# Two-layer graph network on one core: the row-picking one-hots compare two half-precision operands in SBUF

## The reference, cut to what matters

```
def _rel_layer(h, src, dst, etype, norm, V, comp, loop_w, bias, activation):
    c = comp[etype]
    for b in range(num_bases):
        xb = h @ V[b]
        m = m + c[:, b, None] * xb[src]
    agg = segment_sum(m * norm, dst)
    out = agg + bias + h @ loop_w
...
h = maximum(layernorm(x), 0);  x = x + relational layers 0 and 1 of h
h = maximum(layernorm(x), 0);  x = x + gcn layers 0 and 1 of h
```

## Time and profile before

| quantity | value |
|---|---|
| median of 3 runs | 2073.78 us (2073.11 to 2077.47) |
| span of the profiled execution | 2533.6 us |
| PE, DVE, POOL, ACT busy in it | 1943.2, 1535.0, 1411.4, 357.2 us |
| gathers by POOL | 1430 (1312 + 102 + 16) |
| halves of picks by DVE | 268, mean 1815 ns |
| mean granted PE clock | 0.79 |

### The profile page before, as it was taken

How to read it: one execution, slowest core, us unless ns; L and a number is a source line. 1 busy time by engine, 2 the same in 40 slices (tenths; PEclk the granted TensorE clock), 3 DMA queues, 4 the chain that set the end, 5 groups by cost and what they waited for, 6 DMA issues and landing times. The chain is left out here.

```text
span 2533.6 us, 40547 instructions
## 1 busy us (share of the span) xinstructions
PE 1943.2 (77%) x12305; PEld 1396.7 (55%) x12306; DVE 1535.0 (61%) x2202; ACT 357.2 (14%) x869; POOL 1411.4 (56%) x1527
## 2 busy tenths in 40 slices
PE   1577777778777777777748887878878788776898
PEld 1466665556556555655525555555555465554665
DVE  7887778777777777777654445555455455441243
ACT  2111221211121121122200000000000000000110
POOL 5765566656566566656266566566565566566000
PEclk7577777877777777787768788888898789886899
DMA  5232223223223222322221121112232222223354
GB/s 130 58 83 65 66 63 81 68 65 79 66 63 77 65 67 64 80 67 61 58 53 50 47 50 49 48 50 80 66 87 62 53 78 64 76 63 88 108 212 138
DMA packets 194040, 186.56 MB, mean 74 GB/s; under 512 B 109133, under 2 KB 166974, under 8 KB 193947
## 3 DMA queue, kind: packets, MB, share of 16 engines
q0 software_dynamic: 45760, 93.81, 14.9%
q1 hardware_dynamic: 140134, 87.49, 12.1%
q10 hardware_dynamic: 8052, 4.04, 0.6%
HBM read 159.75 MB, written 25.47 MB: 73 GB/s over the span
## 5 line engine op out<-in xcount | busy, mean ns | idle before, releaser
L811 POOL DMA_INDIRECT ring<-h_rows,rel_idx x1312 | 1259.7, 960 | 750.5 <-issue 377.7
L982 DVE TENSOR_TENSOR rel_pick<-rel_src_row,dve_bank 128x1664 bf16<-128x1664 int32 (+1 forms) x268 | 486.4, 1815 | 368.4 <-remote 170.8
L1269 PE MATMUL rel_ps_z<-rel_C,ring 128*128 128x56 f32 x3100 | 484.6, 307 | 134.0 <-issue 123.5
L1269 PEld LDWEIGHTS rel_ps_z<-rel_C,ring 128*128 128x128 f32 x3100 | 477.7, 229 | 171.9 <-issue 163.1
L1213 PE MATMUL rel_ps_p<-rel_h_parts,rel_pick 128*128 128x384 bf16 x1150 | 300.8, 390 | 47.6 <-issue 47.5
L1367 ACT ACTIVATE rel_ZT<-rel_ps_z 128x304 f32 x292 | 114.2, 426 | 1401.6 <-remote 688.4
L1200 PE MATMUL carried<-rel_h_parts,rel_pick 128*128 128x384 bf16 x1100 | 236.9, 367 | 61.9 <-issue 50.8
L1200 PE MATMUL rel_ps_p<-rel_h_parts,rel_pick 128*128 128x384 bf16 x1100 | 227.0, 366 | 60.3 <-issue 25.7
L1357 ACT ACTIVATE rel_A<-rel_ps_a 128x500 f32 x292 | 165.5, 602 | 533.1 <-remote 315.9
L1200 PEld LDWEIGHTS carried<-rel_h_parts,rel_pick 128*128 128x128 bf16 x1100 | 113.1, 106 | 176.1 <-issue 112.9
L1200 PEld LDWEIGHTS rel_ps_p<-rel_h_parts,rel_pick 128*128 128x128 bf16 x1100 | 117.5, 110 | 160.4 <-issue 96.7
(11 more groups left out here) (229 smaller groups left out, 1937.3 us busy)
## 6 DMA issues: line engine op xcount, KB each, us to landing
ring<-h_rows,rel_idx POOLq DMA_INDIRECT x1312
A_slabs<-rel_A SPq DMA_DIRECT2D x25, 800.0 KB
A_slot<-A_slabs SPq DMA_DIRECT2D x25, 800.0 KB, 4.4
early_slot<-A_slabs SPq DMA_DIRECT2D x18, 896.0 KB
rel_types<-edge_types SPq DMA_DIRECT2D x97, 100.0 KB
rel_src_row<-in_src_dram SPq DMA_DIRECT2D x134, 64.0 KB
last_slot<-A_slabs SPq DMA_DIRECT2D x4, 512.0 KB, 5.9
ring<-h_rows,idx_table POOLq DMA_INDIRECT x118
```

Of the source, the lines that this page charges most:

```text
L811: g_.indirect_dma_start(ring[:, s * CHUNK + i, :], None, rows_in, bass.IndirectOffsetOnAxis(ap=idx[which][:, n:n + 1], axis=0)).then_inc(l ...
L982: v.tensor_tensor(pick[:, b0:b0 + n, :], src_row[s][:, :].unsqueeze(1).to_broadcast(shape), node_ids[:, b0:b0 + n].unsqueeze(2).to_broadca ...
L1269: ins = m_.matmul(bank(ps_z[s], NB)[:, :, bass.ds(at[i], TW)], ring[:, first + i, :], C[s][:, i, :, :], start=False, stop=(i == n - 1))
```

## The change

In `prepare`, ACT writes the source numbers less 1562 as half precision (`src_half`; all numbers then lie between -1562 and 1562), and SP stores them in three transfers to a new DRAM tensor `edge_sources`. `src_row` is loaded from there and is half precision. The 25 numbers in PSUM are gone; in their place stands a full table of node numbers less 1562, one half-precision number per element of `pick` (`node_rows`). Its first half is a new tile, its second half lies in `dst_table`. Two DVE instructions fill it once, in group 0 of layer 0. `h_rest` moves out of `dst_table`: into `pick` in layer 0 and into `early_sums` in layer 1. Number, place and order of the picks stay.

```diff
+            sp.wait_ge(src_half_ready, 1)
+            sp.dma_start(t.src_dram[0:full]..., src_half[:, 0:RAW - 1, :]).then_inc(src_out, 16)
+            sp.dma_start(t.src_dram[full:full + rows * P]..., src_half[0:rows, RAW - 1, :]).then_inc(src_out, 16)
+            sp.dma_start(t.src_dram[full + rows * P:E]..., src_half[rows:rows + 1, RAW - 1, 0:tail]).then_inc(src_out, 16)
             sp.wait_ge(type_ready, 1)
...
+            sp.wait_ge(src_out, 48)
...
+            act.wait_ge(srcf_ready, 1)
+            nc.scalar.activation(src_half[:, :, :], src_f[:, :, :], ACT.Copy, bias=-float(MIDDLE)).then_inc(src_half_ready, 1)
             act.wait_ge(type_in, 16)
...
-        src_row, pick = [sb(f"src_row{i}", [P, P], I32) for i in range(sources)], sb("pick", [P, SRC_BLOCKS, P], BF16)
+        src_row, pick = [sb(f"src_row{i}", [P, P], F16) for i in range(sources)], sb("pick", [P, SRC_BLOCKS, P], BF16)
...
-        h_rest = t.dst[:, 0:SPLIT_GROUPS * P].rearrange("p (g n) -> p g n", n=P)
+        h_rest = (flat(pick[:, 0:2 * SPLIT_GROUPS, :]).bitcast(F32) if layer == 0 else t.early[:, 0:SPLIT_GROUPS * P]).rearrange("p (g n) -> p g n", n=P)
...
-                    rows = io["src"].rearrange("(a n) -> a n", a=1)
+                    rows = t.src_dram.rearrange("(a n) -> a n", a=1)
...
-                v.tensor_copy(node_ids, t.node_id[:, :]).then_inc(consts_ready, 1)
...
+            def make_node_rows():
+                for h, (b0, n) in enumerate(PICK_HALVES):
+                    v.tensor_scalar(t.node_rows[h], t.node_id[:, b0:b0 + n].unsqueeze(2).to_broadcast([P, n, P]), -float(MIDDLE),
+                                    None, ALU.add).then_inc(consts_ready, 1)
+                dve.wait_ge(consts_ready, 3)
...
                     v.tensor_tensor(pick[:, b0:b0 + n, :], src_row[s][:, :].unsqueeze(1).to_broadcast(shape),
-                                    node_ids[:, b0:b0 + n].unsqueeze(2).to_broadcast(shape), ALU.is_equal).then_inc(pick_ready, 1)
+                                    t.node_rows[h], ALU.is_equal).then_inc(pick_ready, 1)
```

More of the change, by code:

```diff
@@ L81 @@
 PAD_DST = 4000
+MIDDLE = N // 2
 EPS = 1e-5
@@ L159, in prepare @@
         rest = sb("rest", [RH, 2, 2 * NB], F32)
+        src_half, src_half_ready, src_out = sb("src_half", [P, RAW, P], F16), sem("src_half"), sem("src_out")
         raw_type, type_byte = sb("raw_type", [TYPE_ROWS, TYPE_COLS], I32), sb("type_byte", [TYPE_ROWS, TYPE_COLS], U8)
@@ L211, in _ @@
             sp.dma_start(t.bias_col[:, :], io["L1_gnn_b1"].rearrange("(p a) -> p a", a=1)).then_inc(w_in, 16)
+            sp.wait_ge(src_half_ready, 1)
+            sp.dma_start(t.src_dram[0:full].rearrange("(c q e) -> q c e", q=P, e=P), src_half[:, 0:RAW - 1, :]).then_inc(src_out, 16)
+            sp.dma_start(t.src_dram[full:full + rows * P].rearrange("(q e) -> q e", e=P), src_half[0:rows, RAW - 1, :]).then_inc(src_out, 16)
+            sp.dma_start(t.src_dram[full + rows * P:E].rearrange("(q e) -> q e", q=1), src_half[rows:rows + 1, RAW - 1, 0:tail]).then_inc(src_out, 16)
             sp.wait_ge(type_ready, 1)
@@ L678, in relational_layer @@
         match = [t.ps_c[:, 256 + i * CHUNK * TW:256 + (i + 1) * CHUNK * TW].rearrange("p (i w) -> p i w", w=TW) for i in range(2)]
-        node_ids = t.ps_c[:, 384:384 + SRC_BLOCKS]
         if layer == 0:
@@ L927, in _ @@
             if layer == 0:
-                v.tensor_copy(node_ids, t.node_id[:, :]).then_inc(consts_ready, 1)
                 v.tensor_copy(keys, t.iota[:, :]).then_inc(consts_ready, 1)
-                dve.wait_ge(consts_ready, 2)
+                dve.wait_ge(consts_ready, 1)
                 for m in range(AHEAD):
@@ L1036, in group @@
                             split_rows(split_chains, ((0, 1), (2, 3), (4,))[j])
+                        if is_first and j == 2:
+                            make_node_rows()
                         if j % 2 == 0:
@@ L1960, in program @@
         t.h1_dram, t.h2_dram = dram("h1_rows", (GROUPS * P, D), F32), dram("h2_rows", (GROUPS * P, D), F32)
+        t.src_dram = dram("edge_sources", (E,), F16)
         t.types_dram = dram("edge_types", (E,), U8)
@@ L2001, in program @@
                 with ExitStack() as edges:
+                    t.node_rows = [left(edges, "node_rows", [P, PICK_HALVES[0][1], P], F16)[:, :, :],
+                                   t.dst[:, 0:PICK_HALVES[1][1] * P // 2].bitcast(F16).rearrange("p (b e) -> p b e", e=P)]
                     t.coef = [None, left(edges, "coef1", [P, TILES, NB], F32)]
```

## The result

The changed kernel takes 2101.18 us (median of 4 runs, 2093.49 to 2106.47), the kernel before 2074.43 beside it (4 runs, 2073.11 to 2077.47). The ratio is 1.0119 with an interval of 1.0089 to 1.0148: **27 us slower**. The direction and the range of the forecast held, its size did not: +56 us had been forecast. Two words are used from here on: a *hold* is the time for which a gather of POOL stands still until an operation of DVE is over, and *relief* is the time that DVE has less to do.

The account below looks back on a forecast made before the run. The prediction took POOL's gathers to bound the kernel, with no room in the timed runs. Terms of 41 (layer 1), 14 (layer 0) and 1 us (once-only parts) added 56 to 2073.8, giving 2130 us, range 2028 to 2180.

Parts of the forecast that it names:

- once-only parts: Setup and layer starts: building the table +2 to +4 us, first pick before the split -1.66 us, net +1 us.
- POOL as the bound: Whole run: POOL's gathers, 0.30 us apart, leave POOL no room in the timed runs; chance 0.57 as the forecast.
- sum of 2066: POOL's path: 25.4 before the first gather, 1816 of gathers, 45.9 between layers, 179.1 after the last, against a 2073.8 median.
- The compare itself: DVE's pick halves: doubled rate, 1.02 and 0.96 us instead of 1886 and 1745 ns, freeing 222 us of DVE.
- The price of a hold: POOL's gathers beside pick halves with two SBUF inputs: held 0.79 us per pick, bounds 0 and 105 us in all.
- How much is paid: Share of holds reaching the end: six tenths, 41 of 69 us in layer 1 and 22 of 36 in layer 0.
- Layer 0: Layer 0's 46 picks: +22 us of holds paid, -8 us from a tenth of DVE's 76 us relief, +14 us.
- The spans of the profiled executions: Profiles before and after: spans hardly differ, since PE's gaps cover POOL.
- Rival A: Whole run: PE or DVE is last, POOL has slack, holds cost nothing, relief gains about 40 us: 2034 us; chance 0.24.
- B: POOL's gathers: two-byte operands don't hold them, doubled compare rate without holds: 2067 us; chance 0.08.
- D: DVE's compare: stays at one element per tick and holds gathers for longer: about 2300 us; chance 0.04.
- C: Both layers: PE's waits swallow most holds and layer 0's relief pays for the rest: 2074 us; chance 0.07.

Follow-up runs that it names:

- before_fast: The kernel before, unchanged, profiled on a chip where it takes about 2075 us: span 2071.9 us, layer 0 939.8 us, layer 1 883.6 us.
- half_rows_3: From the kernel before, pick halves after the first two picks compare only 64 of 128 edges, less DVE work without new holds: 2040.9 against 2075.3 us.
- pe_light: From the kernel before, PE multiplies only the even blocks of each pick, the odd ones left out: 2046.1 against 2077.2 us.
- before_again: The kernel before, unchanged, run again on a slower chip (chip 0): timed median 2532.2 us, profiled span 2533.0 us.
- shift_second: From the changed kernel, a DVE filler with one PSUM input ahead of each second pick half in layer 1: 2150.4 us against 2075.9 for the kernel before.
- layer0_only_3: From the changed kernel, layer 1's picks compare against numbers in PSUM again, layer 0 keeps the SBUF table: 2071.0 us against 2076.5 for the kernel before.
- layer1_only_3: From the changed kernel, layer 0's picks compare against numbers in PSUM again, layer 1 keeps the SBUF table: 2102.9 us against 2075.3 for the kernel before.

## Why the prediction was right and wrong

The forecast was +56 = 41 (layer 1) + 14 (layer 0) + 1 (once-only parts). Between the profiled executions came 29.4, 3.9 and 1.4, and 27 between the medians.

**POOL as the bound: right in layer 1, with a flawed proof.** Layer 1 stays at 883 us whether PE or DVE does less, and follows up what holds add to POOL's busy time. But the sum of 2066 hit the median by luck. It took 45.9 us between the layers and 179.1 behind the last gather from the 2533.6 us execution; they are 36.3 and 154 in before_fast. Gathers back to back end the run at 2041 to 2046 us (half_rows_3, pe_light), and in layer 0 DVE and PE took 25 to 32 us more (939.8 against 914.9 and 907.8), which filled the rest. A sum that meets the median within 8 us was taken for proof that nothing else is waited for. The same step put the 459.8 us between profile and median down to profiling, which before_again refutes.

**The compare itself: right.** 1.02 and 0.96 us forecast, 1027 and 948 ns measured; DVE is freed of (1886 + 1743 - 1027 - 948) x 134 = 222 us. The Trainium skill (Vector Engine (DVE) Microarchitecture Reference, 5.1 Performance modes) has a two-source operation with two-byte operands run at the doubled rate, and the trace agrees: 1886 to 1027 ns for 1664 elements.

**The price of a hold: mechanism right, size twice too high.** 0.79 us a pick and 105 us in all were forecast, 53.5 came. This is the step that failed: "a half of length d catches a gather with chance d / 1.25 and holds it for d / 2". There are two reasons. A gather must start behind the half's start and at least 0.15 us ahead of its end, so the chance is (d - 0.19) / 1.25 and the mean hold (d - 0.15) / 2: 0.54 us a pick, 72 us in all. In layer 0 that gives 25 us, and 26.1 were measured (20.8 to 26.1 over three kernels with the same picks). In layer 1 it gives 47, and 27.4 were measured: the phase isn't random. 59 of 88 second halves start 0.12 to 0.38 us behind a gather's start, where they are over before they can hold the next; shift_second took this away and the holds nearly trebled (27.4 to 76.7 us). That the halves are released by PE, and PE by landed gathers (140.1 us of waits), would tie them to POOL's beat; this link is argued, not shown. The Trainium skill (SBUF — State Buffer, Who interferes with whom) infers that a `tensor_tensor` does not stall a DMA whose descriptors GpSimd makes; for these gathers that is contradicted, 121 of 121 were held. A gather also reads its 128 indices from SBUF, and no run here tells whether it is this read or the making of descriptors that stands still.

**How much is paid: wrong, and it hid part of the first error.** Six tenths were forecast on the strength of 254 us "remote"; these are not there in before_fast, and there again in before_again (261.4 us), so they go with the other chips. In layer 1 POOL's busy time grew by 30.8 us and the layer by 29.4, nearly all of it. So 69 us of holds at six tenths, +41, were forecast, and 27.4 paid nearly in full, about +29, came.

**Layer 0: wrong in both terms.** Forecast were +22 and -8. POOL's busy time grew by 28.7, paid in full once POOL is last; and DVE's relief of 76 us gave back about 25 (235.4 - 210.6), not the tenth that was forecast. The prediction looked for the relief in the waits for `coef` (25.6 us). They don't fall (18.8 us in before_fast, 22.2 after); what falls is the wait for the row that L988 copies out, 143.3 us in 46 waits, one for each pick in layer 0, to 88.5, and to 107.9 in half_rows_3, where the layer is 32 us shorter. That wait is in before_fast and not among. Its size alone doesn't measure the path: in pe_light it is 166.1 us and layer 0 is 25 us shorter all the same. That the relief acts through this wait is argued; that it acts is shown. +14 was forecast, +3.9 came.

**The spans of the profiled executions** were to hardly differ. They are 2533.6 and 2104.7 us, since they must come from unlike chips. **Rival A** saw rightly that DVE and PE have a share in layer 0's end, and wrongly that POOL has slack. **B** and **D** are refuted by the held gathers and by 1027 ns. **C**, that both sides cancel, comes true in layer 0 alone (+3.9 us; layer0_only_3 takes 0.27% less than before) and not in layer 1. **The once-only parts** were put at +1. The 1.4 us of setup, change of layers and tail are no measure of them: the setup alone takes 69.6 to 71.5 us over the ten profiles from such chips, 69.6 to 70.8 with the old code and 70.4 to 71.5 with the new. The table's two instructions take 1.88 and 1.13 us; the waits for `coef` grow by 3.4, and layer 0 of layer1_only_3, with the table built and neither holds nor relief, is 3.5 us above before_fast, in the range of +2 to +4 forecast for them. The wait for the split falls from 22.0 to 20.3 us, 1.7 as forecast. Of the marks named for the profile, DVE's busy time fell by 213 us (1530.5 to 1317.4, about 220 forecast), the mean gather rose by 42 ns (up to 80 forecast), and PE's waits for landings rose, as was said for POOL last.

## What to carry to other kernels

A faster instruction can cost time by what it reads: check which neighbour stands still while it runs, and count its cost by the phase of the two and not by chance alone. Where two paths are nearly equal, give the faster form only to as many instructions as the second path needs; a quarter of the halves of one layer turned a loss of 27 us into a gain of 20. Before a profile is used as the account of a timed run, its span must match that run; here 460 us of difference were put down to profiling and carried wrong waits into two terms.

## What the runs showed of the hardware

- A gather that starts up to 0.13 us ahead of a DVE operation with two SBUF inputs, or with it, isn't held (44 of 45); one that starts 0.04 us or more behind the operation's start, and 0.15 us or more ahead of its end, ends 0.81 us after it (121 of 121, within 0.03). With one input in PSUM nothing is held (none of 327).
- An operation with one SBUF input can hold a gather in the same way: the type one-hots (100x1024, bf16 from uint8, 0.75 us) do, to 0.81 us after their end; a sum over 3200 half-precision elements (6.16 us) holds only those that start in its last 0.54 us.
- The compare takes 1886 and 1743 ns with int32 against one PSUM number repeated, and 1027 and 948 ns with two half-precision SBUF inputs.
- The same kernel takes 2524 to 2533 us on two chips and 2075 to 2077 on four, with gathers of the same length (962 and 960 ns) and 0.79 against 0.889 of granted clock; PE's waits with no releaser are 359 us on the slower kind and 6 on the other (at L1269 alone 116.5 and 3.2). The cause stays open.
- Two POOL copies of 0.205 us amid gathers cost 0.21 us together and not 0.41, as part of them takes the place of the 0.30 us between gathers.
